# List scatters spread over GpSimd's waits, two buffers for the list words, and the seventh pair's places made beside the last output products

## The reference, cut to what matters

```python
h = tok_ref(...)                                   # state-space kernel: 16 x 64 rows of 512
h = concatenate([h, txt_ref(x_txt, ...)], axis=1)  # + 16 x 128 rows of an embedding softmax
h = h + attn_ref(layernorm(h), ...)                # Mamba-like layer: in-projection, conv, state, gate, RMS norm, out-projection
h = h + ffn_ref(layernorm(h), ...)                 # mixture of 32 experts, 8 per token
# inside ffn_ref
router_probs = softmax(x @ gate_weight.T)
router_top_value, router_indices = top_k(router_probs, 8)
# the last four choices may be moved to a similar one of the first four
combine = sum(one_hot(rerouted_indices) * routing_weights)
for e in experts: y = y + (silu(g) * u) @ wd[e].T * combine[:, e]
```

## Time and profile before

| | us |
|---|---|
| median of 3 runs | 1774.24 (1768.41 to 1785.33) |
| the profiled execution | 1780.81 |
| its span | 1779.1 |
| layer, to the last scatter's issue | to 1136.55 |
| experts, first instruction to the end of the span | 1146.0 to 1779.1 |
| POOL busy in the list scatters, 192 of them | 219.9, mean 1.145 each |
| PE busy / DVE busy / ACT busy / POOL busy | 1574.6 / 971.2 / 730.3 / 781.5 |
| mean granted TensorE clock | 0.917 |

### The profile page before, as it was taken

The page is one execution under the profiler, slowest core; times in us unless marked ns, Lnnn a source line. Parts: engine busy times, 40 slices in busy tenths (PEclk is TensorE's granted clock), DMA queues, the critical chain, the costliest instruction groups (busy, mean ns, idle before and its releaser), DMA issues. The chain is left out here.

```text
span 1779.1 us, 31373 instructions
## 1 busy us (share of the span) xinstructions
PE 1574.6 (89%) x9263; PEld 1146.1 (64%) x9264; DVE 971.2 (55%) x2325; ACT 730.3 (41%) x1592; POOL 781.5 (44%) x638
## 2 busy tenths in 40 slices
PE   7999999997599999999999670099999999999996
PEld 7999999975477576675766340066655666666564
DVE  5555554523768998889789545034333343433443
ACT  2525253522776765857658100033333333333332
POOL 4230300011042357677675567545544555555554
PEclk9999999988799998998899575599999999999999
DMA  7210000003355352443423110167767777777665
GB/s 267 77 60 1 13 1 13 1 18 134 114 152 143 93 153 77 134 130 93 151 64 90 27 37 2 60 181 190 159 154 188 162 181 167 169 183 182 162 114 92
DMA packets 97703, 195.20 MB, mean 110 GB/s; under 512 B 38391, under 2 KB 46879, under 8 KB 92880
## 3 DMA queue, kind: packets, MB, share of 16 engines
q0 software_dynamic: 36992, 88.26, 23.1%
q1 hardware_dynamic: 60624, 105.78, 19.5%
HBM read 144.15 MB, written 49.84 MB: 109 GB/s over the span
## 5 line engine op out<-in xcount | busy, mean ns | idle before, releaser
L1888 PE MATMUL moe_ps_gu<-moe_wgu,moe_xt 128*128 x960 | 331.9, 489 | 0.0
L1746 POOL DMA_INDIRECT out_h<-moe_yy,moe_idx_s x121 | 190.9, 1578 | 256.2 <-DVE moe_idx_s L1808 117.4
L1016 POOL DMA_INDIRECT scratch_slots<-lay_toki,lay_slot x192 | 219.9, 1145 | 59.0 <-issue 58.1
L1888 PEld LDWEIGHTS moe_ps_gu<-moe_wgu,moe_xt 128*128 128x128 f32 x960 | 173.7, 191 | 96.6 <-issue 1.2
L1785 ACT ACTIVATE moe_sl<-moe_ps_gu 128x192 f32<-128x192 f32 x120 | 39.7, 331 | 365.7 <-PE moe_ps_gu L1888 336.2
L1411 DVE SCALAR_TENSOR_TENSOR lay_xa<-lay_ring,head_cw,lay_xa 128x378 f32<-128x378 f32 (+5 forms) x240 | 141.9, 609 | 54.4 <-ACT lay_xa L1068 46.0
L1197 PE MATMUL lay_ring<-lay_xnt,win_sb 128*128 128x128 f32 (+2 forms) x1152 | 167.6, 292 | 4.3 <-DVE lay_xa L1411 2.0
L1281 PE MATMUL lay_ring<-head_wout,lay_yb 128*128 128x512 f32 x384 | 170.1, 597 | 0.0
L1197 PEld LDWEIGHTS lay_ring<-lay_xnt,win_sb 128*128 128x128 f32 (+2 forms) x1152 | 150.6, 200 | 10.5 <-issue 3.8
L1740 POOL DMA_INDIRECT moe_xg<-scratch_xg,moe_idx_g x123 | 131.4, 1069 | 47.5 <-issue 28.7
L247 POOL TENSOR_TENSOR tok_vv<-tok_w 128x512 f32<-128x512 f32 x16 | 16.6, 1040 | 259.7 <-ACT tok_w L449 225.5
(11 more groups left out here) (290 smaller groups left out, 2961.5 us busy)
## 6 DMA issues: line engine op xcount, KB each, us to landing
lay_m<-scratch_cum SPq DMA_DIRECT2D x16, 1536.0 KB
moe_wgu<-in_wgu SPq DMA_DIRECT2D x32, 768.0 KB
moe_wd<-in_wd SPq DMA_DIRECT2D x32, 384.0 KB
out_h<-lay_hres SPq DMA_DIRECT2D x48, 128.0 KB
scratch_xg<-lay_x SPq DMA_DIRECT2D x48, 128.0 KB
win_sb<-in_win SPq DMA_DIRECT2D x1, 4384.0 KB, 16.3
tok_u_raw<-in_tok_u SPq DMA_DIRECT2D x16, 256.0 KB, 4.5
tok_v_raw<-in_tok_v SPq DMA_DIRECT2D x16, 256.0 KB, 5.1
```

The lines of the kernel that those rows point to most:

```text
L1016: pool.indirect_dma_start(out=a["slots"], out_offset=bass.IndirectOffsetOnAxis(ap=slot[:, j, k:k + 1], axis=0), in_=toki[:, j:j + 1], in_o ...
L1746: pool.indirect_dma_start(out=a["out"], out_offset=bass.IndirectOffsetOnAxis(ap=idx_s[n][:, 0:1], axis=0), in_=yy[n][:], in_offset=None, b ...
L1888: last = mm(ps_gu[b][:], xt[b][:, t], wgu[:, bass.ds(r * KD + t, 1)].rearrange("p o n -> p (o n)"), start=t == 0, stop=t == KD - 1)
```

## The change

Four things change, all in the layer.

1. **Two buffers.** `slot`, `toki` and the semaphore `scat` are doubled, and pair k uses number k % 2. The waits before writing them are for the scatters of pair k - 2 and earlier ones of that number, not of pair k - 1.
2. **Cuts.** The 24 scatters of a late pair are split differently over POOL's turn: 5, 7, 4 and 8 (before 3, 3, 4 and 14) in turns that have a next pair, and 5, 4, 11 and 4 in turn 7.
3. **Pair 6's places.** In turn 7 `router_columns(6)` moves ahead of the residuals of pair 7, and `router_counts(6)` and `router_places(6)` move between the second and the third residual. On PE `places(6)` moves from behind `output(7, 2)` to between `output(7, 1)` and `output(7, 2)`.
4. **The ring's order** follows, so that pair 6's "pl" bank comes ahead of the last output's.

```diff
-        if 0 <= i < PAIRS:
-            order += [("o", i, j) for j in range(N_BLK)]
+        for j in range(N_BLK):
+            if 0 <= i < PAIRS:
+                order.append(("o", i, j))
+            if j == 1 and i == PAIRS - 1:
+                order.append(("pl", i - 1, 0))
...
-        if i - 1 >= PAIRS - 2:
+        if i == PAIRS:
             order.append(("pl", i - 1, 0))
...
                 def list_places(k):
                     pool.wait_ge(slot_done, k + 1)
-                    if k:
-                        pool.wait_ge(scat, k * (3 * TOPK * 16))
+                    if k >= 2:
+                        pool.wait_ge(scat[k % 2], k // 2 * (3 * TOPK * 16))
...
+                    cuts = (0, 5, 12, 16, 3 * TOPK) if pairs(n) else (0, 5, 9, 20, 3 * TOPK)
...
                     if listed_late(w):
-                        fill_lists(0, 3)
+                        fill_lists(w, cuts[0], cuts[1])
                     if pairs(i):
                         square_sums(i)
...
                     if listed_late(w):
-                        fill_lists(3, 6)
+                        fill_lists(w, cuts[1], cuts[2])
                     if pairs(i):
                         pool.wait_ge(ssv_done, i + 1)
                         nc.gpsimd.tensor_tensor(rr[:], ssv[:], mhalf[:], ALU.pow).then_inc(rr_done, 1)
                     if listed_late(w):
-                        fill_lists(6, 10)
+                        fill_lists(w, cuts[2], cuts[3])
...
                     if listed_late(w):
-                        fill_lists(10, 24)
+                        fill_lists(w, cuts[3], cuts[4])
                     if listed_early(r):
                         list_places(r)
-                        fill_lists(0, 24)
-                pool.wait_ge(scat, PAIRS * 3 * TOPK * 16)
+                        fill_lists(r, 0, 3 * TOPK)
+                for n in range(2):
+                    pool.wait_ge(scat[n], PAIRS // 2 * 3 * TOPK * 16)
...
                         output(i, 0)
                         square_columns(i)
                         output(i, 1)
+                    if listed_early(r) and pairs(i):
+                        places(r)
...
-                    if listed_early(r):
+                    if listed_early(r) and not pairs(i):
                         places(r)
...
-                    if k:
-                        dve.wait_ge(scat, k * (3 * TOPK * 16))
-                    own.mark(v.tensor_copy(toki[:], tokf[:]))
+                    if k >= 2:
+                        dve.wait_ge(scat[k % 2], k // 2 * (3 * TOPK * 16))
+                    own.mark(v.tensor_copy(toki[k % 2][:], tokf[:]))
...
+                    if listed_early(r):
+                        router_columns(r)
                     if pairs(n):
                         state_matrix(n, 0)
                     for j in range(N_BLK):
                         if pairs(i):
                             residual(i, j)
+                        if listed_early(r) and j == 1:
+                            router_counts(r)
+                            router_places(r)
                     for k in range(N_XT):
                         if pairs(n):
                             x_dt(n, k)
-                    if listed_early(r):
-                        router_columns(r)
                     if pairs(i):
                         routed_shift(i)
-                    if listed_early(r):
-                        router_counts(r)
-                        router_places(r)
```

More of the change, by code:

```diff
@@ L793, in build_layer @@
         slotf = s.sb("slotf", [P, 3, TOPK])
-        slot = s.sb("slot", [P, 3, TOPK], I32)
-        toki = s.sb("toki", [P, 3], I32)
+        slot = [s.sb(f"slot{n}", [P, 3, TOPK], I32) for n in range(2)]
+        toki = [s.sb(f"toki{n}", [P, 3], I32) for n in range(2)]
         gf = s.sb("gf", [P, 2])
@@ L877, in build_layer @@
         w_out = s.sem("w_out")
-        scat = s.sem("scat")
+        scat = [s.sem(f"scat{n}") for n in range(2)]
         counted = s.sem("counted")
@@ L1006, in list_places, with fill_lists @@
                     pool.wait_ge(slot_done, k + 1)
-                    if k:
-                        pool.wait_ge(scat, k * (3 * TOPK * 16))
+                    if k >= 2:
+                        pool.wait_ge(scat[k % 2], k // 2 * (3 * TOPK * 16))
                     nc.gpsimd.tensor_tensor(slotf[:], posk[:], on[:], ALU.add).then_inc(listed, 1)
                     pool.wait_ge(listed, k + 1)
-                    own.step(nc.gpsimd.tensor_copy(slot[:], slotf[:]))
-                def fill_lists(first, last):
+                    own.step(nc.gpsimd.tensor_copy(slot[k % 2][:], slotf[:]))
+                def fill_lists(i, first, last):
                     for q in range(first, last):
@@ L1016, in fill_lists @@
                         pool.indirect_dma_start(
-                            out=a["slots"], out_offset=bass.IndirectOffsetOnAxis(ap=slot[:, j, k:k + 1], axis=0),
-                            in_=toki[:, j:j + 1], in_offset=None,
-                            bounds_check=P * SLOT_COLS - 1, oob_is_err=False).then_inc(scat, 16)
+                            out=a["slots"], out_offset=bass.IndirectOffsetOnAxis(ap=slot[i % 2][:, j, k:k + 1], axis=0),
+                            in_=toki[i % 2][:, j:j + 1], in_offset=None,
+                            bounds_check=P * SLOT_COLS - 1, oob_is_err=False).then_inc(scat[i % 2], 16)
                 project_text(0)
```

## The result

| | before | after |
|---|---|---|
| median of 10 runs on one chip | 1772.7 us (1767.9 to 1785.3) | 1790.3 us (1780.1 to 1800.9) |
| ratio, with its 95% interval | 1 | 1.0082 (1.0055 to 1.0109) |
| the profiled execution | 1780.81 | 1782.69 |

The changed kernel is slower by 0.8% where 13 us less were forecast. The two profiled executions took nearly the same time: before's is one of its slowest, after's one of its fastest. So the traces show what is different, but not the whole of the loss.

What follows compares the result with a forecast made beforehand. PE sets the pace in turns 1 to 5, POOL's queue of scatters bounds the tail. Tail 13.1 us saved, middle 0: median 1774.24 - 13.1 = 1761 us, range 1744 to 1778, the forecast's own 1753 to 1769.

Steps and rivals of the forecast that it cites:

- POOL's queue in the tail: Tail: scatters fill POOL's waits, `rstd` starts at 1052.5, pair 6's scatters end at 1091.2, the last at 1123.4; 13.1 us saved.
- Does DVE deliver pair 7's addresses by 1091.2?: Tail, DVE: pair 7's addresses come at 1089.7, in time by 1.5 us; each further microsecond late comes off the gain.
- The chain's own length: Tail, DVE: from the end of pair 7's logits to its addresses, reckoned as 24.3 us, plus 0.4.
- a sign that it is wrong: Tail: the prediction is wrong if POOL waits for `slot_done` of pair 7.
- the third rival: Tail: pair 7's router takes over, its chain 6 us later than reckoned; saving 8.6, time 1766 us; chance 0.12.
- the rivals on the slower side: Middle turns: early gates fall on DVE's chain, 1775.5 us, chance 0.16; the one rival marked the slower side.
- 1062.64, plus 2.4 for the late `rstd`: Tail: PE's end of pair 7's logits before, plus the delay; the chain on DVE starts from 1065.0.
- Turns 2 to 6: Middle of the layer: six scatters leave each turn's end, gates begin earlier; +2.1 - 2.0, 0 within its errors.
- `rr` delayed the first residual: Turns 2 and 4: four more scatters ahead of `rr` start the first residual 1.1 us later; together +2.1.
- The additions to `macc`: Turns 4 and 6, DVE: with earlier gates the additions finish 0 to 2.0 us sooner in each.
- the second rival: Turns 3 to 6: early gates stretch DVE's step sums by 3.07 us each; 14.4 lost against 13.1, 1775.5 us; chance 0.16.
- This wait absorbs it: Middle turns: DVE's 3.13 us wait for PE's state products absorbs the step sums' 3.07 us stretch; taken as nothing.

Runs made afterwards that it cites:

- quiet_chain: Changed kernel, but pair 6's 24 scatters wait until pair 7's addresses are made; ratio to the kernel before 1.0097 (1.0068 to 1.0127).
- after_again: Changed kernel once more without an edit, for a second profile; ratio to the kernel before 1.0021 (0.9989 to 1.0053), median 1797.0 us.
- group 1: One chip's runs after_again, mid_old_cuts, old_cuts and cuts_alone; new against old splits of turns 2 to 6, with two buffers: 1797.0 against 1803.9 us.
- group 3: One chip's runs: tail_cuts and cuts_alone again (1774.8 and 1770.9 us), cuts_alone with gates held (0.9890), mid_old_cuts with a pause before pair 6's scatters (0.9973).
- mid_old_cuts: Changed kernel, but turns 2 to 6 split the scatters 3, 3, 4 and 14 as before; ratio to the kernel before 1.0090, 1803.9 us.
- old_cuts: Changed kernel, but all turns split the scatters 3, 3, 4 and 14; ratio to the kernel before 1.0025, 1793.7 us.
- tail_cuts: Kernel before, with the new split 5, 4, 11, 4 in turn 7 alone; ratio to the kernel before 0.9929, run again 0.9948.
- cuts_alone: Kernel before, with the new splits in all turns and nothing else; ratio to the kernel before 0.9956, run again 0.9910.
- places_late: Changed kernel without parts 3 and 4: two buffers and new splits, pair 6's places late; ratio to the kernel before 1.0011, 1795.5 us.
- pause_and_gate: Changed kernel with pause_first's wait, and each pair's first gate held until DVE made the next step sums; ratio to the kernel before 0.9845, 1742.4 us.
- pause_first: Changed kernel, but in turn 7 POOL waits ahead of `rstd` until twenty scatters have landed; ratio to the kernel before 0.9915, 1778.1 us.
- stores_late: Changed kernel, but SP's stores of pair 7's x2 wait until pair 7's addresses are made; ratio to the kernel before 0.9995, 1793.5 us.
- quiet_logits: Changed kernel, but pair 6's 24 scatters wait for PE's last product of pair 7's logits; ratio to the kernel before 1.0014 (0.9980 to 1.0048).
- group 5: One chip's two runs: pause_and_gate (0.9845, 1742.4 us), and the kernel before with new splits and gates held (0.9848, 1742.1 us).

## Why the prediction was wrong, point by point

**POOL's queue in the tail: right.** The prediction counts from the scatters and square sums of turn 7. Pair 5's list, which stands just ahead of them on POOL, is started in after at 1012.81, and in before at

```profile
1018.14 0.23 POOL L1009 TENSOR_TENSOR lay_slotf<-lay_posk,lay_on 128x24 f32<-128x24 f32 x1 [4.34 <-DVE lay_on L1551]
```

so that after is 5.3 us earlier there. Forecast, shifted by that: `rstd` at 1047.2, the end of pair 6's scatters at 1085.9. Measured: 1046.93 and 1084.64.

**"Does DVE deliver pair 7's addresses by 1091.2?": here it failed.** The chain's own length was right (23.9 us in quiet_chain, forecast 24.3). Its start was wrong. The prediction took DVE to begin when PE's products end, and read the 13.22 us wait in front of `toki` as the only thing between them. A second wait of 7.55 us stood in its shadow, and it grew to 14 us in after, and to 16 + 16 in after_again, when the scatters no longer stopped for landings. The addresses came 20.2 us later than forecast (1104.6 against 1089.7 - 5.3). Of this PE's products are 0.6, the hold on the logits 14.3, and later hand-overs of the chain 5.3, the 3.2 on the similarity products among them. POOL waited 20.19 us, which the prediction had named as a sign that it is wrong, and its last scatter was issued by 1136.47 against 1118.1.

**The rivals.** The mechanism was the third rival's, pair 7's router in the tail, priced at 6 us of lateness where 20 and more came; at 0.12 and 1766 us it was the right place at the wrong size. None of the rivals on the slower side named it. The term that was mis-sized is the start of the chain, "1062.64, plus 2.4 for the late `rstd`", to which nothing was added for the hand-over from PE to DVE; it measured 7.55 us in before and 14.3 in after.

**The range**, 1744 to 1778, missed 1790.3 because the doubt about the tail had only 4.5 us in it (13.1 against 8.6).

**Turns 2 to 6: zero forecast, little measured, made of larger terms.** `rr` delayed the first residual by 0.78 us in four turns (forecast 1.1 in two). The additions to `macc` took 2.16 in turn 4 instead of 3.82, but 2.17 in turn 5 instead of 0.98. L1406 took 4.1 us in turns 3 to 6 instead of 0.60, just as the second rival had it; here the rule of the Trainium skill's page "GPSIMD Engine Reference", section "Key points", on the shared SBUF interfaces is borne out. "This wait absorbs it" was wrong at least in part: with the gates held the kernels were 5.2 us (not clear of noise) and 8.3 us faster. Holding them also takes the stretch out of turns 0 to 2, where the kernel before has it, so not all of it is the change's. The splits of the middle as a whole gained 6.9 us in group 1, and 3.9, not clear of noise, in group 3; through which step is not shown.

**Part by part**, by ratio: the split of turn 7 alone -0.5 to -0.7% with one buffer, and +0.6% with two (mid_old_cuts against old_cuts); the splits of turns 2 to 6 a further -0.7% with two buffers, and with one nothing sure (-0.4% on one chip, +0.3% between tail_cuts and cuts_alone, of different chips); two buffers on top of the splits +0.6 to +1.0% (places_late against the two runs of cuts_alone, of different chips); the early places nothing that can be told. The parts do not add up, since what one of them is worth depends on whether the logits are held. Once the holds are gone, buffers and early places shorten the tail by 2.8 us (208.0 against 210.8), which the time doesn't show (1742.4 against 1742.1 us, five executions each). The profile of pause_and_gate is of no help there: it is of the slowest of the five, 1754.4 us, and the experts took 646.1 us in it against 635.1.

## What to carry to other kernels

Before a wait is removed, look at what ended in its shadow: for every semaphore behind it, the end of its producer and the start of its consumer, since a wait hides every other wait that ends sooner. A row of scatters without a break is not free for the hand-overs of other engines; ahead of a short chain of many of them, a pause of 3 us on the issuing engine gave back 15 (pause_first against stores_late). And where filling a side engine's idle time makes its next job start beside the critical engine's work, try holding that job back on a semaphore.

## What the runs showed of the hardware that was not expected

- **Semaphores raised late beside scatters.** The time from the end of PE's last logits product to DVE's first step was under 0.15 us in every profile without a hold, and 7.3 to 22.8 us in the others. In DVE's table of quiet_logits 23 of 34 steps waited 1.0 to 1.3 us each, and seven 0.5 to 0.6, where before has no wait at all. In the middle of the layer, PE's semaphore for the one-hots came late as well: mostly by 2.3 to 3.8 us in turns 2 to 6 with the new splits, by at most 2.3 with the old ones, and not at all in the two profiles of group 5. Holding the scatters back takes it away, and so does a pause of 2.6 to 3.2 us ahead; taking SP's stores away doesn't. Of the nine holds on the logits seven ended 0.9 to 4.5 us after the last scatter of a row (1070.19 and 1069.28 in before, 1096.08 and 1091.62 in after_again), two in the middle of one. What in the chip does this was not found.
- **A held hand-over depends on the execution.** The same kernel had 14 us and 16 + 16 us. Its executions spread over 21 us in each group, but those of the kernel before spread over 8 to 31, so the spread by itself says nothing.
- **A gate of 3.4 us on POOL stretches a small DVE step from 0.6 to 4.1 us**, with its end just behind the gate's (694.84 and 694.41 in turn 3 of after), as if it waited for the gate rather than ran slower. By the record the step had begun 0.23 us ahead of the gate (690.73 and 690.96). POOL's `rr` took 3.15 us when DVE's long step on the decays had begun ahead of it; it took 1.79 in the same turns before, and 0.88 undisturbed.
